# A two-block transformer kernel on one Trainium2 core: where the next heads' score units stand among a head's transposed units

## The reference, cut to what matters

```
q = (x @ Wq.T)  32 heads of 16;  k, v  8 heads of 16;  rope on q and k
scores = q k^T / sqrt(16), causal mask over t = 1024
attn = softmax(scores);  ctx = attn @ v;  out = ctx @ Wo.T
```

## Time and profile before

| what | value |
|---|---|
| median of 3 runs | 810.98 us (810.4 to 812.01) |
| the profiled execution's own time | 809.74 us |
| its span, first to last instruction | 807.7 us |
| mean granted TensorE clock, of 2.4 GHz | 0.968 |
| TensorE matmul, busy | 732.0 us, 91% |
| VectorE, ScalarE, GpSimd, busy | 480.2, 323.1, 337.8 us |

### The profile page before, as it was taken

The page is one execution under the profiler, slowest core; times in us unless marked ns, Lnnn a source line. Parts: engine busy times, 40 slices in busy tenths (PEclk is TensorE's granted clock), DMA queues, the critical chain, the costliest instruction groups (busy, mean ns, idle before and its releaser), DMA issues.

```text
span 807.7 us, 10131 instructions
## 1 busy us (share of the span) xinstructions
PE 732.0 (91%) x3654; PEld 440.6 (55%) x3654; DVE 480.2 (59%) x715; ACT 323.1 (40%) x536; POOL 337.8 (42%) x277
## 2 busy tenths in 40 slices
PE   4897999889999999879999999799778999997998
PEld 2443333333343332148678888454447788875886
DVE  3758777677778776246565457767785333336311
ACT  3311266566766766751245311454243333222100
POOL 0227993785475553671165332213532222124300
PEclk9998899999999999999999999999789999998999
DMA  9442624150550500230033200213000110111111
GB/s 312 151 116 68 141 79 90 68 115 15 102 108 10 115 3 2 95 99 7 0 83 100 65 1 1 72 43 65 34 6 27 53 52 26 52 52 52 40 66 39
DMA packets 24110, 52.99 MB, mean 66 GB/s; under 512 B 4252, under 2 KB 8100, under 8 KB 23044
## 3 DMA queue, kind: packets, MB, share of 16 engines
q1 hardware_dynamic: 24068, 52.44, 23.7%
HBM read 45.63 MB, written 6.60 MB: 65 GB/s over the span
## 4 chain that ended last, share of the span: by engine, by line
PE 68%; DVE 12%; issue 8%; POOL 6%; ACT 3%; DMA 1%; SPq 1%; ACTq 0%; DVEq 0%; POOLq 0%
PE ps L862 65%; DVE mxp L1755 3%; PE ps L879 2%; ACT pr L1411 1%; DMA rq<-in_mask 1%; POOL wsum L2165 1%; DVE st L1597 1%; POOL pr L2181 1%; POOL x L2275 1%; DVE xnb L1621 1%; DVE x L1943 1%; DVE arena L1640 1%; PE ps L1028 1%; POOL wmr L2163 1%; POOL rs L2094 1%
## 5 line engine op out<-in xcount | busy, mean ns | idle before, releaser
L862 PE MATMUL ps<-arena 128*128 128x512 f32 (+1 forms) x1416 | 332.1, 395 | 7.9 <-DVE arena L1640 4.2
L862 PEld LDWEIGHTS ps<-arena 128*128 128x128 f32 (+1 forms) x1416 | 264.8, 188 | 68.2 <-DVE arena L1640 6.1
L1755 DVE TENSOR_REDUCE mxp<-ps 128x2 f32<-128x1024 f32 (+3 forms) x160 | 172.6, 1114 | 55.0 <-PE ps L862 53.3
L1411 ACT ACTIVATE pr<-ps 128x512 f32<-128x512 f32 x288 | 162.3, 596 | 86.5 <-PE ps L862 84.0
L862 PE MATMUL ps<-Qst,Kst 99*128 99x512 bf16 x288 | 103.0, 388 | 9.5 <-ACT pr L1411 7.4
L862 PE MATMUL ps<-Kst,Qst 96*128 96x512 bf16 (+3 forms) x384 | 101.5, 336 | 7.6 <-DVE mxp L1755 5.8
L2181 POOL TENSOR_TENSOR pr<-pr,cap 128x512 int32<-128x512 int32 x56 | 70.7, 1278 | 32.8 <-ACT pr L1411 32.6
L862 PE MATMUL ps<-pr,vr 128*32 128x512 f32 x576 | 76.8, 606 | 5.0 <-POOL pr L2181 4.3
L862 PEld LDWEIGHTS ps<-Kst,Qst 96*128 96x128 bf16 x384 | 35.8, 99 | 66.3 <-DVE mxp L1755 26.8
L862 PEld LDWEIGHTS ps<-Qst,Kst 99*128 99x128 bf16 x288 | 26.6, 98 | 82.3 <-ACT pr L1411 60.9
L2280 POOL TENSOR_TENSOR arena<-raw,arena 128x1024 fp32r<-128x1024 f32 x11 | 27.1, 2467 | 84.3 <-ACT arena L1477 84.3
(11 more groups left out here) (197 smaller groups left out, 821.2 us busy)
## 6 DMA issues: line engine op xcount, KB each, us to landing
wmr<-in_wmr SPq DMA_DIRECT2D x8, 1280.0 KB, 11.3
raw<-in_w SPq DMA_DIRECT2D x16, 512.0 KB, 3.3
Qst<-q_parts SPq DMA_DIRECT2D x42, 128.0 KB
q_parts<-qparts SPq DMA_DIRECT2D x3, 768.0 KB, 3.7
x<-in_x SPq DMA_DIRECT2D x8, 256.0 KB, 6.4
wm<-in_wm SPq DMA_DIRECT2D x4, 512.0 KB, 7.4
raw<-in_up SPq DMA_DIRECT2D x8, 256.0 KB, 2.6
raw<-in_down SPq DMA_DIRECT2D x8, 256.0 KB, 2.6
```

The source lines that it names most:

```text
L862: return nc.tensor.matmul(outp, lhs, rhs, start=start, stop=stop, skip_group_check=True)
L1411: A(pr[:, k % PRING, :], ps[:, 4 + k % 2, :], ACT.Exp, scale=float(DH) ** -0.5).then_inc(exp_done, 1)
L1755: V.tensor_reduce(mxp[:, kh, g0:g0 + heads, i].rearrange("p (b e) -> p b e", e=per), units, AXX, ALU.max)\
```

## The change

```diff
--- before.py
+++ after.py
@@ -291,12 +291,6 @@
 CTX_AT = AHEAD + 2
 
 
-def reduce_cost(s):
-
-    i, _, heads, kh = SUNITS[s]
-    return 160 + heads * width(i, kh)
-
-
 def slots_before(h, s=0):
 
 
@@ -320,28 +314,26 @@
 VT_AT = 11
 
 
+SCORES_AT = (0, 1, 4, 5, 6, 9, 10, 13, 13, 15, 17, 18, 20, 22)
+CONTEXT_AT = 3
+MAXIMA_AT = 25
+AHEAD_AT = (26, 29, 29, 31, 33, 34)
+assert len(SCORES_AT) == NS - AHEAD and len(AHEAD_AT) == AHEAD
+assert SCORES_AT[CTX_AT - AHEAD - 1] < CONTEXT_AT < SCORES_AT[CTX_AT - AHEAD]
+
+
 def body_steps(nxt, nxt2, ctx):
 
 
     todo = []
     if nxt:
-        for s in range(AHEAD, NS):
-            if s == CTX_AT and ctx:
-                todo.append(("ctx", -1, None, 1400))
-            todo.append(("s", 1, s, reduce_cost(s)))
-        todo.append(("max", 1, None, 1600))
-        todo.append(("mod", 1, None, 300))
-    elif ctx:
-        todo.append(("ctx", -1, None, 1400))
+        todo += [(SCORES_AT[s - AHEAD], "s", 1, s) for s in range(AHEAD, NS)]
+        todo += [(MAXIMA_AT, "max", 1, None), (MAXIMA_AT, "mod", 1, None)]
+    if ctx:
+        todo.insert(CTX_AT - AHEAD if nxt else 0, (CONTEXT_AT, "ctx", -1, None))
     if nxt2:
-        todo += [("s", 2, s, reduce_cost(s)) for s in range(AHEAD)]
-    total = sum(x[3] for x in todo)
-    out, sofar = [], 0
-    for what, d, s, cost in todo:
-        step = sofar * NTU // max(total, 24000)
-        out.append((max(step, 3) if what == "ctx" else step + 2 * (what == "max"), what, d, s))
-        sofar += cost
-    return out
+        todo += [(AHEAD_AT[s], "s", 2, s) for s in range(AHEAD)]
+    return todo
```

## The result

| | before | after |
|---|---|---|
| median of 6 runs each, in turn on one chip, us | 811.5 (809.64 to 813.55) | 805.11 (803.26 to 807.26) |
| profiled execution, us | 809.74 | 803.79 |
| its span, us | 807.7 | 801.7 |

The ratio of after to before is 0.9923, 95% interval 0.9896 to 0.9949: faster by 4 to 8 us. The sign is as forecast; the time lies 0.1 us above the range (798.5 to 805.0), and the gain is two thirds of the forecast.

The account below looks back on a forecast made before the run. TensorE bounds the kernel (68% of the chain), with thinly spread waits. Gains of 1.1 (head 0), 3.2 (heads 1 and 2), 4.1 (3 to 5) and 1.2 (6) sum to 9.6 us, giving 801.4 us, range 798.5 to 805.0.

Parts of the forecast that it names:

- Steady heads: Heads 3 to 5: a head takes 30.3 us instead of 31.67, gaining 1.36 each, 4.1 together.
- T26's wait: Heads 3 to 5: the 0.64 us wait ahead of transposed unit 26 goes, filled by maxima turn and `mod_step`.
- two release rules: TensorE: unit k + 2 starts at least 1.08 us behind unit k; score unit s + 2 at least 1.91 behind s.
- Head 6: Head 6, no units ahead: maxima turn and `mod_step` fill the same wait, 29.18 us instead of 30.42, gain 1.2.
- The race of L1769: Rival, heads 2 to 5: L1769 starts behind GpSimd's weighing, costing 1.8 us a head, 808.6 us; chance 0.10.
- Head 0, the release: Head 0: VectorE's copy that releases unit 1 of head 2 comes at 121.3 to 121.8, as before.
- Head 0, what follows the release: From the copy's release to unit 0 of head 1: 6.28 us instead of 7.37, a gain of 1.1.
- the price of a fall: Each fall of TensorE's clock to the 1.2 GHz level costs 1.34 us, as in head 1 before.
- Heads 1 and 2, the move of GpSimd's work: GpSimd's gapless 18.05 us up to round 0 of head 2 move along with head 1's `mod_step`.
- 1.46 is what counts: Head 1's `mod_step` comes 1.46 us sooner, and round 0 of head 2, which waits for GpSimd, gains that.
- Head 2 from round 0 on: Head 2 behind round 0 gains 1.72 us, 0.36 more than a whole steady head.
- The clock falls in the new waits: Rival, heads 0 and 2: the clock falls behind waits up to 2.9 and 2.1 us, 804.1 us; chance 0.20.

Follow-up runs that it names:

- `h0_fill`: The changed kernel with head 0's six units ahead moved to steps 26, 31, 32, 33, 34, 35: 803.48 us, ratio 0.9894 to the kernel before.
- `lora_late`: The changed kernel with GpSimd's low-rank weight splitting moved from behind head 1 to ahead of head 7: 800.39 us, ratio 0.9864 to the kernel before.

## Why the prediction was right in part and wrong in part

- **Steady heads: right, to 0.05 us a head.** Round 0 came 6.77 behind T0 (6.79 forecast), round 3 16.24 (16.31), the maxima turn 20.94 (20.95), the next head 30.26 (30.31). The 0.42 in the context turn stayed and T26's wait went. All of it comes from two release rules read from one head of before. (Thirteen of the 23 steps differ, not twelve; nothing hangs on it.)
- **Head 6: right.** 29.05 for 29.18; the gain is 1.37 against 1.2.
- **The race of L1769: right that it is not lost**, here 0.01 us ahead. The copy comes 2.16 behind the maxima turn, as before.
- **Head 0, the release: right.** GpSimd's last tensor operation of the rotation starts at 117.22 instead of 118.69, so this execution runs 1.47 ahead; on the times of before the copy releases at 121.25, against 121.3 to 121.8. The maxima turn came some 3 us sooner and gained nothing, since the chain of VectorE's short operations paid for three of GpSimd's instead of one (below).
- **Head 0, what follows the release: wrong.** "the new order has 6.28. Gain 1.1 us" took the full clock. It measured 8.96, with the clock at 0.50 from 119 to 125: 2.68 us for one fall, a term that the sum had at nothing, and twice the 1.34 that I had as the price of a fall, since this fall lasted twice as long. That is the largest single error of this execution. The wait was 3.72 and not 2.9. My reading is that time won ahead of a fixed release went into it: the first waits of the head shrank to 0.47 and 0.27 (1.35 in the earlier trace rows), and the clock did not fall at 99 (0.63 there from 98 to 102 before, now 1.00). `h0_fill` shows the release standing still: short wait, full clock, 5.47 us behind the copy for 5.5 expected.
- **Heads 1 and 2, the move of GpSimd's work: wrong in the mechanism.** The step was "GpSimd then works without a gap until round 0 of head 2 ...; the whole 18.05 us move along" with `mod_step`, "1.46 is what counts". `mod_step` did come 2.36 sooner behind T0 (24.25 for 26.61), but the weighing only 0.39 sooner and round 0 0.59 (44.07 for 44.66), which is 0.87 us short of the 1.46. (The 2.36 is more than 1.46 because the clock did not fall at 149 this time.) I had asked what is late next for TensorE, and not for GpSimd: the load of `wmr`, on no row that I had read, had landed only 0.3 us ahead of the weighing's start before. Head 1's own gain (35.72 to 33.40) was paid back as a longer wait in head 2.
- **Head 2 from round 0 on: wrong by the clock.** 23.52 was forecast, 25.10 measured, with the clock at 0.50 from 174 to 176: 1.58 us, more than the move of GpSimd's work lost. Where the clock did not fall behind round 0 (`lora_late`), it took 23.50.
- **The rivals.** "The clock falls in the new waits", 804.1, is what came about, joined by the load that no rival held. That its figure is within 1 us of the measured 805.11 is in part luck: it has no load in it, and prices each fall at 1.34 for 2.68 and 1.58. Its chance of 0.20 was argued from which waits had and had not brought a fall in one execution, and the runs show that one execution can't tell. In the kernel with new steps in heads 3 to 6 alone, heads 0 to 2 are those of before, and round 0 of head 2 waits 2.48 us (before 2.45); this time the clock fell behind it (its table of stretches):

```profile
174.00:176.00 2.00, 2.00 (x9) 0.24 (x10) 0.00 (x0) 0.00 (x0) 2.00 (x2) 0.50 0.97 271
```

In the profile of before it is 1.00 from 174 to 179. In that execution heads 0 to 2 took 107.52 us together, in before 106.43, in the changed kernel 106.93. By the means given further up, heads 0 to 2 take some 108.0 us before: the profile of before was a lucky one for their terms, by about 1.6 us.

What stays open: why a wait of one length brings a fall in one execution and not in the next, and how much head 0's new steps cost or bring on average. The kernels with and without them differ by less than the runs scatter, and the two means of head 0 by 0.1 us.

## What to carry to other kernels

A step table is worth its full replay only where TensorE's own rules end the waits; ahead of a wait that another engine or a load ends, what is won only lengthens that wait. So before a releasing event is moved, list everything that its successor needs, and when each lands: one that lands 0.3 us sooner than the event caps the gain at 0.3. Where a release can't move, put independent work ahead of it and keep the wait short, for the low clock that came with the longer waits cost 1.6 and 2.7 us here, on top of them.

## What the runs showed of the hardware that I had not expected

**Short VectorE operations pay for GpSimd one by one.** VectorE's timeline at the maxima turn of head 0:

```profile
113.89 2.25 DVE L1761 TENSOR_TENSOR mt<-mt,mparts 32x128 f32<-32x128 f32 x1
116.18 1.03 DVE L1762 CAST mparts<-mt 32x128 bf16<-32x128 f32 x1
117.25 2.24 DVE L1763 TENSOR_TENSOR mparts<-mt,mparts 32x128 bf16<-32x128 f32 x1
119.41 0.30 DVE L1767 COPY full<-ps 128x160 f32<-128x160 f32 x1
```

GpSimd's timeline of the same time:

```profile
113.87 2.13 POOL L2130 TENSOR_TENSOR qacc<-qacc,qparts 128x1024 f32<-128x1024 f32 x1
116.09 1.05 POOL L2057 TENSOR_SCALAR qparts<-qacc 128x1024 bf16<-128x1024 f32 x1
117.22 2.12 POOL L2130 TENSOR_TENSOR qparts<-qacc,qparts 128x1024 bf16<-128x1024 f32 x1
```

Each of the three starts 0.02 to 0.09 us behind one of GpSimd's and ends behind it: 5.52 us for what takes 1.30 in a steady head (0.28, 0.72, 0.30), where the cast still ends just behind one of GpSimd's; at 121.00 in the kernel before, with GpSimd idle, the cast took 0.21. The Trainium skill, on the page SBUF — State Buffer, section Who interferes with whom, states an exclusive lock by which the first to start keeps the shared port for its whole instruction; the rows agree, and show that a dependent chain loses the race anew at every link.

**The clock's fall is not a property of the program.** Behind waits of 1.36 and 1.48 it fell in one execution (new steps but for head 0); behind the like waits, 1.36 and 1.48, it did not in another (heads 3 to 6 alone, 1.00 at 97 to 101 and at 121 to 125). Behind the twelve waits of 2.84 to 4.34 us in heads 0 and 2 of nine kernels it fell every time, in six of them while TensorE still waited, and those six were the long falls. The Trainium skill, on the page TensorE: Matmul & The Clock Gate, in Part 1 on the clock gate, says of a kernel's start that the count of slow matmuls varies from run to run, since the monitor's window runs free of the kernel. These executions show the like in the middle of a kernel.
